# Top-16 attention scores as whole float32 products on half arrays, with the first values moved behind the first scores

## The chip, the cores and the metric

The kernel runs on one core of a Trainium2 chip. The metric is the device time of one execution in microseconds (us). PE is TensorE (PEld its weight loads), DVE is VectorE, ACT is ScalarE, POOL is GpSimd, SP is SyncE, which here only starts DMAs.

## The reference, cut to what matters

The whole computation is a small network on 1250 nodes and 512 features: a graph layer, a causal attention layer with experts, a second graph layer, and last a top-16 attention layer. Only the last one is touched:

```
x = x + (pos + pos_b)                      # depthwise taps along the rows
q, k, v = split(x @ qkv_w.T + qkv_b)       # 8 heads of 64
logits = einsum("bmd,bpd->bmp", q * scale, k)          # 1250 x 1250 for each head
_, idx = top_k(logits, 16)
attn = softmax(einsum("bmd,bmkd->bmk", q * scale, k[idx]))
out = einsum("bmk,bmkd->bmd", attn, v[idx]) @ wo_w.T + wo_b
```

Which 16 keys a row takes hangs on the exact order of its scores, so the scores need float32 precision.

## The kernel before

`top_layer` (from L1143) is the last of the kernel's stages and begins at about 1094 us of the profiled span. Its engines run programs of their own, which wait for each other on semaphores. After the taps, the q and k columns of the first pair of heads are projected (L1340), six chunks that ACT puts away in `QO` and `KT` (`keep_qk`, L1526). Then 80 tiles follow, n = 0 to 79: 8 heads of 10 tiles, and a tile is 128 queries against all 1250 keys. Two heads make a pair i; head `half` of the pair lies in rows 0 to 63 or 64 to 127 of `QO` and `KT`, since a head has 64 features. For each tile:

- PE `scores(n)` (L1373) makes 128 x 1250 scores in three PSUM banks; two sets of three banks alternate, so tile n needs ACT and DVE to be done with tile n-2.
- DVE `largest(n)` (L1678): the 8 largest, the scores without them, the next 8, the scores without those (four passes over 1250 columns, L1683 to L1691). After every second tile it takes a reciprocal of two sums (L1696), for which it waits on ACT's `total` (L1589).
- ACT: exp of the scores (L1581), exp of what is left (L1587), the sum (L1591); POOL subtracts the two (L1285), which leaves 16 weights a row. DVE may not overwrite its buffer of tile n before POOL has subtracted tile n-2.
- PE turns the weights by ten 128x128 transposes in three groups (L1406), each of which waits until ACT has put the group before it away (L1608), and for every second tile multiplies two tiles by the values (`weigh`, L1421, float32, output 64 wide, the two tiles on the two column halves of the array by turns).

PE, ACT and POOL walk the tiles in a written order. In PE's order round n is: first group of `turn(n-2)`, `scores(n+1)`, then a quarter of a job, second group, a quarter, third group, the rest. At every odd n there may be one job of the next pair (`work_at`, L1155): five q/k jobs of four 512-column products each, then three values jobs (four, four and two tiles of 128 rows; each is four products and one product with a single row for the bias, L1347 and L1349), 8 jobs in the 10 double rounds of a pair, three times. In the last 20 tiles only four light jobs are left. `weigh` comes in even rounds. I call two tiles (an odd round and the even one behind it) a round pair.

The scores need float32 precision, and the kernel gets it by splitting. k is staged twice over the 128 rows and split in a rounded part `kh` and a rest `kl`; q is stacked as rest and rounded part in `qs`. Then 128-row products of the type float32r over `kh` and over `kl` give the scores: 6 matmuls (512, 512, 226 columns, twice). The copies come by DMA (SP, L1231 to L1238, 4 of 320 KB for each head), and POOL splits them (`stage`, five operations for each head). For the first head that happens ahead of all scores: DVE splits k (L1673, L1675), POOL q. Meanwhile PE computes the first pair's values (L1368).

In the profile a float32 matmul leaves two MATMUL records, a transpose or a float32r matmul one.

Of the kernel before, what the change touches and what calls it, by code (L numbers as in the profile page):

```python
# [12 lines left out]
F32 = mybir.dt.float32  # L13
# [1129 lines left out]
def top_layer(nc, m, io, space, raw_qk, raw_v, taps, qb, s_ahead, ahead_done, out):  # L1143

    TN = H * NT
    LEFT, EXS, TOPS, PTS = 2, 3, 4, 4
    groups = pieces(NP)
# [7 lines left out]
    work_at, kept_after, jobs_before = {}, {}, {}  # L1155
    for i in range(1, HP):
        for v, job in enumerate(qk_jobs):
            work_at[2 * NT * (i - 1) + 1 + 2 * v] = ("qk", i, job)
        for v, ts in enumerate(v_groups):
            work_at[2 * NT * (i - 1) + 11 + 2 * v] = ("v", i, ts)  # L1160
# [8 lines left out]
    qk_kept = [None] + [kept_after[2 * NT * (i - 1) + 1 + 2 * (len(qk_jobs) - 1)] for i in range(1, HP)]  # L1169
    v_kept = [len(v_groups)] + [kept_after[2 * NT * (i - 1) + 11 + 2 * (len(v_groups) - 1)] for i in range(1, HP)]  # L1170
    qkv_jobs = jobs_before[61]

    with ExitStack() as ctx:
        s = Stage(nc, m, ctx, "tl")
        (s_zn, s_w_turned, s_w_kept, s_x_turned, s_x_kept, s_edge, s_tapped, s_mid, s_conv, s_first, s_first_kept,
         s_job, s_job_kept, s_wo_in, s_staged_k,
         s_fetched_0, s_fetched_1, s_staged, s_scored, s_max, s_negm, s_read, s_max2, s_topped, s_exp, s_rest,
         s_sum, s_inv, s_blank, s_probs, s_turned, s_kept, s_weighed, s_drained, s_normed, s_biased,
         s_projected, s_final, s_stored) = s.signals(
            "zn w_turned w_kept x_turned x_kept edge tapped mid conv first first_kept job job_kept wo_in staged_k "  # L1180
            "fetched_0 fetched_1 staged scored max negm read max2 topped exp rest sum inv blank probs turned kept "
# [11 lines left out]
        qs = space("tl_qs", 86016, [P, 2, NP], F32R)  # L1193
        kh = space("tl_kh", 96256, [P, 2, NP], F32R)
        kl = space("tl_kl", 106496, [P, 2, NP], F32R)
        qh = space("tl_qh", 116736, [P, NP], F32R)
# [18 lines left out]
        def logits(n):  # L1215
            return banks[:, 3 * (n % 2):3 * (n % 2) + 3, :].rearrange("p b c -> p (b c)")
# [10 lines left out]
        def _(sp):  # L1227
            sp.wait_ge(s_first_kept, 6)
            for i in range(HP):
                for half in range(2):  # L1230
                    r = slice(half * DH, (half + 1) * DH)  # L1231
                    if i:
                        sp.wait_ge(s_job_kept, qk_kept[i])
                        sp.wait_ge(s_scored, (2 * i + half - 1) * NT)
                    for arrived, rows in ((kl, KT[r, i % 2:i % 2 + 1, :]), (qs, QO[r, i:i + 1, :])):
                        for to in range(2):
                            sp.dma_start(arrived[to * DH:(to + 1) * DH, half:half + 1, :].bitcast(F32), rows
                                         ).then_inc(s_fetched[half], 16)  # L1238
                    if (i, half) == (3, 0):
                        sp.wait_ge(s_job, qkv_jobs)  # L1240
                        sp.dma_start(raw_wo[:, :, :], rows_of(io["L1_ffn_wo_w"])).then_inc(s_wo_in, 16)
            for half in range(2):
                sp.wait_ge(s_fetched[half], 64 * HP)
# [8 lines left out]
        def _(pool):  # L1252
            upper, lower = slice(0, DH), slice(DH, P)

            def stage(hi, step):

                half = hi % 2
                if step == (2 if hi == 0 else 0):
                    pool.wait_ge(s_fetched[half], 64 * (hi // 2) + 64)
                    if hi >= 2:  # L1260
                        pool.wait_ge(s_scored, (hi - 1) * NT)
                if step == 0:
                    op = pool.tensor_copy(kh[:, half, :], kl[:, half, :].bitcast(F32))
                elif step == 1:
                    op = pool.tensor_tensor(kl[:, half, :], kl[:, half, :].bitcast(F32),
                                            kh[:, half, :].bitcast(F32), ALU.subtract)
                elif step == 2:
                    op = pool.tensor_copy(qh[lower, :], qs[lower, half, :].bitcast(F32))
                elif step == 3:
                    op = pool.tensor_tensor(qs[lower, half, :], qs[lower, half, :].bitcast(F32),  # L1270
                                            qh[lower, :].bitcast(F32), ALU.subtract)
                else:
                    op = pool.tensor_copy(qs[upper, half, :], qs[upper, half, :].bitcast(F32))
                op.then_inc(s_staged, 1)
                pool.wait_ge(s_staged, 5 * hi + step - 1)

# [24 lines left out]
            for step in (2, 3, 4):  # L1301
                stage(0, step)
            for n in range(TN + 4):
# [6 lines left out]
                hi, step = (n + 8) // NT, (n + 8) % NT  # L1310
                if 0 < hi < 2 * HP and step < 5:
                    stage(hi, step)
# [5 lines left out]
        def _(pe):  # L1318
# [49 lines left out]
            for v, ts in enumerate(v_groups):  # L1368
                if v >= 2:
                    pe.wait_ge(s_job_kept, v - 1)  # L1370
                project_v(banks[:, 7 - v % 2, :], 0, ts).then_inc(s_job, 1)
# [25 lines left out]
            def turn(n, g):  # L1397
                if g == 0:
                    pe.wait_ge(s_probs, n + 1)
                    if n == 0:  # L1400
                        pe.wait_ge(s_job_kept, len(v_groups))
# [856 lines left out]
```

## Time and profile before

| | us |
|---|---|
| median of 3 runs | 1689.25 (1688.99 to 1690.77) |
| the profiled execution | 1686.05 |
| its span, first to last instruction | 1684.2 |
| first DVE pass over scores | 1146.81 |
| start of DVE's tile 79 | 1630.6 |
| mean granted TensorE clock | 0.966 |

The profiled execution is 1.85 us longer than its span and 3.2 us shorter than the median. The stretch that the change touches reaches from 1129 us to the end. A timeline row is a run of like instructions: start, time from the first start to the last end, engine, line, out<-in, rows*columns of the array, count, and in brackets the idle time before it with what ended it. The recorded end of a matmul lies behind the start of the next, since they are pipelined: for the pace, compare starts.

### The profile page before, as it was taken

How to read it: one execution, taken by the hardware profiler on the slowest of the kernel's cores; microseconds unless marked ns; L12 is line 12 of the kernel's file. 1: busy time of each engine (PE TensorE's matmuls, PEld its weight loads, DVE VectorE, ACT ScalarE, POOL GpSimd, SP SyncE). 2: the span in 40 equal slices, each digit the busy share in tenths (PEclk: the TensorE clock that was granted, in tenths of full speed). 3: DMA queues.
4: the chain of work that ended last, by engine and by line, in shares of the span. 5: the costliest groups of instructions: out<-in, count | busy, mean ns of one | idle time of the engine just before them, and what ended most of it. 6: DMA issues, size and time to landing. Idle time of an engine off the chain costs nothing. (4 is left out here: it accounts for less than half of the span.)

```text
span 1684.2 us, 22128 instructions
## 1 busy us (share of the span) xinstructions
PE 1486.9 (88%) x8227; PEld 928.2 (55%) x8227; DVE 1027.9 (61%) x2001; ACT 723.4 (43%) x1396; POOL 541.6 (32%) x399
## 2 busy tenths in 40 slices
PE   4888988997878789999999899777999999998778
PEld 2444534445666654454546545455776776776554
DVE  6999233327777721113223324748999999999981
ACT  4442013225565621111111220235778778778771
POOL 0113200015565410000000060007876667577550
PEclk9999989999999999999999999889999999999999
DMA  6001000025212050000000200011101100120001
GB/s 232 1 1 79 0 1 1 0 63 158 57 39 56 9 204 24 0 0 0 1 0 0 76 1 0 1 31 33 32 1 32 32 13 20 33 53 5 1 1 61
DMA packets 28570, 57.01 MB, mean 34 GB/s; under 512 B 7904, under 2 KB 12644, under 8 KB 28208
## 3 DMA queue, kind: packets, MB, share of 16 engines
q1 hardware_dynamic: 27152, 53.03, 11.5%
q10 hardware_dynamic: 1312, 2.56, 0.4%
q8 instruction: 68, 1.11, 0.3%
q14 instruction: 38, 0.31, 0.1%
HBM read 28.77 MB, written 5.84 MB: 21 GB/s over the span
## 5 line engine op out<-in xcount | busy, mean ns | idle before, releaser
L1285 POOL TENSOR_TENSOR tl_ex<-tl_ex,tl_left 128x1250 f32<-128x1250 f32 x80 | 209.8, 2622 | 37.0 <-ACT tl_left L1587 32.9
L1126 DVE SCALAR_TENSOR_TENSOR X<-ex_ps_x,g,X 128x512 f32<-128x512 f32 x80 | 59.9, 750 | 192.6 <-PE ex_ps_x L1019 192.6
L1406 PE MATMUL tl_banks<-identf,tl_ex 128*128 128x128 f32 x800 | 139.4, 290 | 42.1 <-ACT tl_pt L1608 25.6
L1608 ACT COPY tl_pt<-tl_banks 128x512 f32<-128x512 f32 (+1 forms) x200 | 108.1, 541 | 83.8 <-PE tl_banks L1406 80.8
L992 PE MATMUL ex_ps_h<-yt,w 128*128 128x512 f32 (+1 forms) x384 | 143.8, 529 | 0.0
L1406 PEld LDWEIGHTS tl_banks<-identf,tl_ex 128*128 128x128 f32 x800 | 90.0, 144 | 97.3 <-ACT tl_pt L1608 44.3
L1019 PE MATMUL ex_ps_x<-w,hid 128*128 128x512 f32 (+1 forms) x320 | 143.1, 599 | 0.0
L1072 ACT ACTIVATE hid<-ex_ps_h,b 128x512 f32<-128x512 f32 (+1 forms) x48 | 29.1, 608 | 242.2 <-PE ex_ps_h L992 242.2
L1899 POOL TENSOR_TENSOR lo<-xn,hi 128x512 f16<-128x512 f32 x5 | 5.9, 1186 | 379.5 <-ACT hi L1989 379.5
L1587 ACT ACTIVATE tl_left<-tl_left,tl_negm 128x1250 f32<-128x1250 f32 x80 | 107.5, 1343 | 29.2 <-DVE tl_left L1691 28.8
L1683 DVE MAX8 tl_m<-tl_banks 128x8 f32<-128x1250 f32 x80 | 116.3, 1454 | 5.7 <-PE tl_banks L1383 5.6
L1689 DVE MAX8 tl_m<-tl_left 128x8 f32<-128x1250 f32 x80 | 117.1, 1464 | 2.8
L1687 DVE MATCH_REPLACE8 tl_left<-tl_m,tl_banks 128x1250 f32<-128x1250 f32 x80 | 116.0, 1450 | 0.0
L1691 DVE MATCH_REPLACE8 tl_left<-tl_m,tl_left 128x1250 f32<-128x1250 f32 x80 | 115.6, 1445 | 0.0
L992 PEld LDWEIGHTS ex_ps_h<-yt,w 128*128 128x128 f32 x384 | 74.5, 195 | 65.8 <-issue 65.6
L1581 ACT ACTIVATE tl_ex<-tl_banks,tl_negm 128x1250 f32<-128x1250 f32 x80 | 104.7, 1309 | 2.4 <-DVE tl_left L1687 1.3
L1421 PE MATMUL tl_banks<-tl_pt,tl_V 128*64 128x128 f32 x1600 | 104.8, 278 | 0.0
L1019 PEld LDWEIGHTS ex_ps_x<-w,hid 128*128 128x128 f32 (+1 forms) x320 | 60.3, 189 | 74.0 <-issue 73.9
L1421 PEld LDWEIGHTS tl_banks<-tl_pt,tl_V 128*64 128x64 f32 x1600 | 85.7, 137 | 14.2 <-issue 14.2
L264 DVE TENSOR_SCALAR hot_m<-ruler,ends 128x240 f16<-128x240 f16 x323 | 92.6, 287 | 0.2 <-issue 0.2
L1340 PE MATMUL tl_banks<-tl_ct,tl_wt 128*128 128x512 f32 (+1 forms) x192 | 82.0, 554 | 9.3 <-DVE tl_ct L1658 6.2
L624 PE MATMUL ca_banks<-wqkv,ht 128*128 128x512 f32 x160 | 76.6, 625 | 12.7 <-DVE ht L804 12.7
(272 smaller groups left out, 2935.5 us busy)
## 6 DMA issues: line engine op xcount, KB each, us to landing
kl<-KT SPq DMA_DIRECT2D x16, 320.0 KB, 4.4
qs<-QO SPq DMA_DIRECT2D x16, 320.0 KB, 5.8
tl_kl<-tl_KT SPq DMA_DIRECT2D x16, 320.0 KB, 4.3
tl_qs<-tl_QO SPq DMA_DIRECT2D x16, 320.0 KB, 5.7
w<-in_L_ffn_W SPq DMA_DIRECT2D x8, 512.0 KB
w<-in_L_ffn_W SPq DMA_DIRECT2D x4, 1024.0 KB, 9.7
at_kept<-AT SPq DMA_DIRECT2D x1, 3200.0 KB, 10.9
AT<-at_kept SPq DMA_DIRECT2D x1, 3200.0 KB, 18.3
```

Of the source, the lines that this page charges most:

```text
L992: mm = pe.matmul(h_bank(u)[:, 0:w], w1[e][:, k, j * P:(j + 1) * P], yt[:, G % 2, k, 0:w], start=(k == 0), stop=(k == KD - 1))
L1019: mm = pe.matmul(x_bank(v)[0:rows(t), :], hid[:, (EX * G + e) % HIDS, j, r * P:r * P + rows(t)], w2[:, 2 * e + j, :], start=(j == 0), stop ...
L1285: pool.tensor_tensor(ex[:, n % EXS, 0:N], ex[:, n % EXS, 0:N], left[:, n % LEFT, :], ALU.subtract).then_inc(s_probs, 1)
L1406: mm = pe.transpose(ps_t[:, b * P:(b + 1) * P], ex[:, n % EXS, a + b * P:a + (b + 1) * P], m.identf[:, :])
L1421: mm = pe.matmul(ps_o[u * DH:(u + 1) * DH, 0:P], V[:, h // 2 % 2, k, h % 2 * DH:(h % 2 + 1) * DH], pt[:, (2 * j + u) % PTS, k * P:(k + 1) ...
L1581: act.activation(ex[:, n % EXS, 0:N], logits(n)[:, 0:N], ACT.Exp, bias=negm[:, n:n + 1]).then_inc(s_exp, 1)
L1587: act.activation(lf, lf, ACT.Exp, bias=negm[:, n:n + 1]).then_inc(s_rest, 1)
L1608: act.copy(pt[:, n % PTS, a:a + w], ps_t[:, 0:w]).then_inc(s_kept, 1)
L1683: dve.max(m8[:, n % TOPS, 0:8], logits(n)[:, 0:N]).then_inc(s_max, 1)
L1687: dve.match_replace(lf, m8[:, n % TOPS, 0:8], logits(n)[:, 0:N], TAKEN).then_inc(s_read, 1)
L1689: dve.max(m8[:, n % TOPS, 8:16], lf).then_inc(s_max2, 1)
L1691: dve.match_replace(lf, m8[:, n % TOPS, 8:16], lf, TAKEN).then_inc(s_topped, 1)
```

## The change

The scores are whole float32 matmuls with 64 rows, straight from `QO` and `KT`. Three matmuls a tile: keys 369 to 880 (512 columns) on the half of the array in which the head does not lie, from copies `qd` and `kd` that SP fetches crosswise for a pair at once (4 DMAs for a pair, two slots), and keys 0 to 368 and 881 to 1249 (369 columns each) on the head's own half. Each goes to a bank of its own. The first three tiles (`ALONE`) take all three matmuls on the own half and so need no copy. Splitting on POOL and DVE, and `kh`, `kl`, `qs`, `qh` are gone. The values of the first pair stand behind the scores in rounds 0 to 2, and the jobs of pair 1 begin at round 3 where they began at round 1; the later jobs keep their rounds.

```diff
+    ALONE = 3
+    SIDE = (N - BANK) // 2
...
+        at = 2 * NT * (i - 1) + (3 if i == 1 else 1)
+        for job in qk_jobs:
+            work_at[at] = ("qk", i, job)
+            at += 2
...
+            return banks[:, 3 * (n % 2):3 * (n % 2) + 3, :].rearrange("p b c -> p (b c)")[:, BANK - SIDE:BANK - SIDE + N]
...
+                if i:
+                    sp.wait_ge(s_job_kept, qk_kept[i])
+                if i >= 2:
+                    sp.wait_ge(s_scored, 4 * NT * (i - 1))
+                for copy, rows in ((kd, KT[:, i % 2:i % 2 + 1, :]), (qd, QO[:, i:i + 1, :])):
+                    for half in range(2):
+                        sp.dma_start(copy[(1 - half) * DH:(2 - half) * DH, i % 2:i % 2 + 1, :],
+                                     rows[half * DH:(half + 1) * DH, :, :]).then_inc(s_fetched[i % 2], 16)
...
-            for step in (2, 3, 4):
-                stage(0, step)
...
-                if 0 < hi < 2 * HP and step < 5:
-                    stage(hi, step)
...
                 if n == 0:
-                    pe.wait_ge(s_staged_k, 2)
-                pe.wait_ge(s_staged, 5 * (n // NT) + 3)
+                    pe.wait_ge(s_first_kept, 6)
+                if n >= ALONE:
+                    pe.wait_ge(s_fetched[i % 2], 64 * (i // 2) + 64)
...
-                for part in (kh, kl):
-                    for a, w in pieces(N):
-                        mm = pe.matmul(logits(n)[:, a:a + w], qs[:, half, t * P:(t + 1) * P],
-                                       part[:, half, a:a + w], start=(part is kh), stop=(part is kl))
-                mm.then_inc(s_scored, 1)
+                for other, a, b in ((1, SIDE, SIDE + BANK), (0, 0, SIDE), (0, SIDE + BANK, N)):
+                    if n < ALONE:
+                        other = 0
+                    at = (half + other) % 2
+                    r = slice(at * DH, (at + 1) * DH)
+                    q, k = (qd[r, i % 2, :], kd[r, i % 2, :]) if other else (QO[r, i, :], KT[r, i % 2, :])
+                    mm = pe.matmul(logits(n)[:, a:b], q[:, t * P:(t + 1) * P], k[:, a:b], start=True, stop=True)
+                    if a:
+                        mm.then_inc(s_scored, 1)
...
                 if n + 1 < TN:
                     scores(n + 1)
+                if n < len(v_groups):
+                    first_v(n)
                 if n in work_at:
...
                 if n < TN:
                     exponentials(n)
+                if n < len(v_groups):
+                    keep_first_v(n)
...
-            dve.wait_ge(s_fetched[0], 64)
-            dve.tensor_copy(kh[:, 0, :], kl[:, 0, :].bitcast(F32)).then_inc(s_staged_k, 1)
-            dve.wait_ge(s_staged_k, 1)
-            dve.tensor_tensor(kl[:, 0, :], kl[:, 0, :].bitcast(F32), kh[:, 0, :].bitcast(F32), ALU.subtract
-                              ).then_inc(s_staged_k, 1)
```

On PE at the first tiles, the program of before goes from the last projection of q and k through all of the values (L1347 with 128x128 outputs, L1349 the bias) to the scores of tiles 0, 1 and 2. Its last rows there:

```order
L1347 MATMUL tl_banks<-tl_wt,tl_ct 128x128 x4
L1349 MATMUL tl_banks<-v_b,ones 128x128
L1383 MATMUL tl_banks<-tl_kh,tl_qs 128x512 x2
L1383 MATMUL tl_banks<-tl_kh,tl_qs 128x226
L1383 MATMUL tl_banks<-tl_kl,tl_qs 128x512 x2
L1383 MATMUL tl_banks<-tl_kl,tl_qs 128x226
```

The changed program there, from the last projection of k to the first values (L1314 projects q and k, L1363 makes scores, L1321 and L1323 values):

```order
L1314 MATMUL tl_banks<-tl_ct,tl_wt 128x256 x8
L1363 MATMUL tl_banks<-tl_KT,tl_QO 128x512
L1363 MATMUL tl_banks<-tl_KT,tl_QO 128x369 x2
L1363 MATMUL tl_banks<-tl_KT,tl_QO 128x512
L1363 MATMUL tl_banks<-tl_KT,tl_QO 128x369 x2
L1321 MATMUL tl_banks<-tl_wt,tl_ct 128x128 x4
L1323 MATMUL tl_banks<-v_b,ones 128x128
```

The scores of tiles 0 and 1 moved ahead of the ten tiles of values; four of those stand between the scores of tiles 1 and 2, four behind tile 2's, two behind tile 3's.

In the middle, PE's order in an odd round with a q or k job, in the program of before:

```order
L1406 MATMUL tl_banks<-identf,tl_ex 128x128 x4
L1383 MATMUL tl_banks<-tl_kh,tl_qs 128x512 x2
L1383 MATMUL tl_banks<-tl_kh,tl_qs 128x226
L1383 MATMUL tl_banks<-tl_kl,tl_qs 128x512 x2
L1383 MATMUL tl_banks<-tl_kl,tl_qs 128x226
L1340 MATMUL tl_banks<-tl_ct,tl_wt 128x512
L1406 MATMUL tl_banks<-identf,tl_ex 128x128 x4
```

and in the changed one:

```order
L1386 MATMUL tl_banks<-identf,tl_ex 128x128 x4
L1363 MATMUL tl_banks<-tl_kd,tl_qd 128x512
L1363 MATMUL tl_banks<-tl_KT,tl_QO 128x369 x2
L1314 MATMUL tl_banks<-tl_ct,tl_wt 128x512
L1386 MATMUL tl_banks<-identf,tl_ex 128x128 x4
```

The place in the round is the same; only the matmuls that make the scores differ, and the rows of the array that they take.

## Rows read from the trace of the kernel before

**Rows 1.** Chain of waits, 1128 to 1150 us: start, us, what
```profile
1128.91 0.48 ACT tl_KT L1532
...
1129.41 0.47 SPq L1237
...
1131.63 6.25 DMA tl_qs<-tl_QO
...
1138.00 1.84 POOL tl_qh L1268
...
1139.91 4.03 POOL tl_qs L1270
...
1143.99 1.25 POOL tl_qs L1273
...
1145.38 1.40 PE tl_banks L1383 x6
...
1146.81 1.48 DVE tl_m L1683
```

**Rows 2.** Groups of DVE, 1146.8 to 1637 us: busy, mean ns, idle before
```profile
L1683 DVE MAX8 tl_m<-tl_banks 128x8 f32<-128x1250 f32 x80 | 116.3, 1454 | 5.7 <-PE tl_banks L1383 5.6
...
L1696 DVE RECIPROCAL tl_inv<-tl_rsum 128x2 f32<-128x2 f32 x39 | 6.1, 157 | 6.8 <-ACT tl_e L1591 6.8
```

**Rows 3.** Timeline of DVE: start, us, line, what, idle before it
```profile
1195.18 1.46 DVE L1683 MAX8 tl_m<-tl_banks 128x8 f32<-128x1250 f32 x1
...
1207.22 1.46 DVE L1683 MAX8 tl_m<-tl_banks 128x8 f32<-128x1250 f32 x1
...
1236.06 1.45 DVE L1691 MATCH_REPLACE8 tl_left<-tl_m,tl_left 128x1250 f32<-128x1250 f32 x1
1239.49 0.17 DVE L1696 RECIPROCAL tl_inv<-tl_rsum 128x2 f32<-128x2 f32 x1 [1.99 <-ACT tl_e L1591]
```

**Rows 4.** Timeline of PE, one round with a q or k job
```profile
1195.01 0.65 PE L1392 MATMUL tl_banks<-identf,tl_inv 128*64 128x128 f32 x4
1195.59 1.98 PE L1340 MATMUL tl_banks<-tl_ct,tl_wt 128*128 128x512 f32 x4
...
1197.77 0.81 PE L1383 MATMUL tl_banks<-tl_kh,tl_qs 128*128 128x512 f32 x3
1198.41 0.73 PE L1383 MATMUL tl_banks<-tl_kl,tl_qs 128*128 128x512 f32 x3
1198.99 0.60 PE L1406 MATMUL tl_banks<-identf,tl_ex 128*128 128x128 f32 x4
1199.51 1.31 PE L1421 MATMUL tl_banks<-tl_pt,tl_V 128*64 128x128 f32 x20
...
1209.52 0.81 PE L1383 MATMUL tl_banks<-tl_kh,tl_qs 128*128 128x512 f32 x3
```

**Rows 5.** Timeline of PEld: weight loads in that round
```profile
1204.14 0.73 PEld L1340 LDWEIGHTS tl_banks<-tl_ct,tl_wt 128*128 128x128 f32 x4 [0.27 <-ACT tl_ot L1617]
```

**Rows 6.** Timeline of PE, one round with a values job
```profile
1223.67 0.81 PE L1383 MATMUL tl_banks<-tl_kh,tl_qs 128*128 128x512 f32 x3
...
1230.05 1.16 PE L1347 MATMUL tl_banks<-tl_wt,tl_ct 128*128 128x128 f32 x8
1231.14 0.48 PE L1349 MATMUL tl_banks<-v_b,ones 1*128 1x128 f32 x2
1231.55 0.66 PE L1406 MATMUL tl_banks<-identf,tl_ex 128*128 128x128 f32 x4
...
1237.81 0.81 PE L1383 MATMUL tl_banks<-tl_kh,tl_qs 128*128 128x512 f32 x3
```

**Rows 7.** Timeline of PE while the staging runs
```profile
1130.11 1.16 PE L1347 MATMUL tl_banks<-tl_wt,tl_ct 128*128 128x128 f32 x8
...
1131.61 1.16 PE L1347 MATMUL tl_banks<-tl_wt,tl_ct 128*128 128x128 f32 x8
```

**Rows 8.** Busy time by stretch: PE, PEld, DVE, ACT, POOL, granted clock
```profile
1267.30:1387.80 120.50, 114.52 (x882) 85.92 (x880) 116.23 (x128) 94.62 (x177) 82.69 (x59) 0.99 0.09 19
```

More of the change, by code:

```diff
@@ L1155, in top_layer @@
     work_at, kept_after, jobs_before = {}, {}, {}
+    qk_done = [None]
     for i in range(1, HP):
[L1157 to L1160, printed above, removed]
+        at = 2 * NT * (i - 1) + (3 if i == 1 else 1)
+        for job in qk_jobs:
+            work_at[at] = ("qk", i, job)
+            at += 2
+        qk_done.append(at - 2)
+        for ts in v_groups:
+            work_at[at] = ("v", i, ts)
+            at += 2
     for b in range(KD):
@@ L1168, in top_layer @@
             evictions += len(work_at[n][2]) if work_at[n][0] == "qk" else 1
[L1169 to L1170 removed]
+    qk_kept = [None] + [kept_after[n] for n in qk_done[1:]]
     qkv_jobs = jobs_before[61]
@@ L1175, in top_layer @@
         (s_zn, s_w_turned, s_w_kept, s_x_turned, s_x_kept, s_edge, s_tapped, s_mid, s_conv, s_first, s_first_kept,
-         s_job, s_job_kept, s_wo_in, s_staged_k,
-         s_fetched_0, s_fetched_1, s_staged, s_scored, s_max, s_negm, s_read, s_max2, s_topped, s_exp, s_rest,
+         s_job, s_job_kept, s_wo_in,
+         s_fetched_0, s_fetched_1, s_scored, s_max, s_negm, s_read, s_max2, s_topped, s_exp, s_rest,
          s_sum, s_inv, s_blank, s_probs, s_turned, s_kept, s_weighed, s_drained, s_normed, s_biased,
          s_projected, s_final, s_stored) = s.signals(
-            "zn w_turned w_kept x_turned x_kept edge tapped mid conv first first_kept job job_kept wo_in staged_k "
-            "fetched_0 fetched_1 staged scored max negm read max2 topped exp rest sum inv blank probs turned kept "
+            "zn w_turned w_kept x_turned x_kept edge tapped mid conv first first_kept job job_kept wo_in "
+            "fetched_0 fetched_1 scored max negm read max2 topped exp rest sum inv blank probs turned kept "
             "weighed drained normed biased projected final stored")
@@ L1229, in _ @@
             for i in range(HP):
[L1230 to L1241, printed above, removed]
+                if i:
[6 more added lines that the diff above has]
+                                     rows[half * DH:(half + 1) * DH, :, :]).then_inc(s_fetched[i % 2], 16)
+                if i == 3:
+                    sp.wait_ge(s_job, qkv_jobs)
+                    sp.dma_start(raw_wo[:, :, :], rows_of(io["L1_ffn_wo_w"])).then_inc(s_wo_in, 16)
             for half in range(2):
-                sp.wait_ge(s_fetched[half], 64 * HP)
+                sp.wait_ge(s_fetched[half], 64 * HP // 2)
             sp.wait_ge(s_wo_in, 16)
@@ L1252, in _ @@
         def _(pool):
[L1253 to L1275, printed above, removed]
             def negate(n):
@@ L1543, in keep_job @@
                     if i >= 2:
-                        for half in range(2):
-                            act.wait_ge(s_fetched[half], 64 * (i - 1))
+                        act.wait_ge(s_scored, 4 * NT * (i - 1))
                     for name, c in what:
```

20 lines of the change are left out of this document (8 added, 12 removed).

## Prediction

> **What bounds the kernel now.** I read the chain of waits first, then DVE's groups, then the timelines. The chain [rows 1] shows what stands between the projections and the 80 tiles: ACT puts the last piece of k away until 1129.39, SP issues copies, they land at 1137.88, POOL splits q until 1145.24, PE makes the first scores (1.40), and DVE starts at 1146.81. From then on DVE is the pace: 80 tiles of four passes with 5.6 us of idle at the very start and only 6.8 us at the reciprocals [rows 2]. Undisturbed, two tiles take DVE 1207.22 - 1195.18 = 12.04 us [rows 3]. But PE is close behind: 114.5 of 120.5 us busy over the second pair of heads, at a granted clock of 0.99, the 2.4 GHz level [rows 8]. A round pair with a q or k job takes PE 1209.52 - 1197.77 = 11.75 us, 0.27 of it a wait for ACT [rows 4, 5], so 11.48 of work. One with a values job of four tiles takes 1237.81 - 1223.67 = 14.14, which is 2.1 more than DVE's 12.04 [rows 6]. There DVE does wait: 1.99 us ahead of the reciprocal at 1239.49, since ACT's sum stands behind copies that wait for PE [rows 3]. That is one of six such waits, two for each block of jobs, 2.3 a block.
>
> **The change part by part.**
>
> *The start.* SP's copies, POOL's 1.84 + 4.03 + 1.25 us and DVE's splitting leave the path. Scores of tile 0 can begin at 1129.4: 0.11 weights (half of the 0.20 switch below), then 1250 columns in two records each, all on one half. Price of a column: four records of 512 columns last 1.98, four of 128 last 0.65 [rows 4], so 1.33 us for 1536 columns more, 0.87 ns; at two cycles of the 2.4 GHz level it would be 0.83. I take 0.84: 2.10 us. With 0.19 from the last start to DVE's, DVE begins at about 1131.8 instead of 1146.81: **-15.0 us**. Bounds -14.8 (0.87 ns) and -15.1. The copies for tile 3 still land at about 1137.9 and are wanted 17 us after DVE's start, so they are hidden with 11 us to spare; SP has nothing else queued. Later pairs' copies are issued when k of the pair is put away, eight tiles (48 us) ahead. DVE and POOL drop work otherwise off the path: no gain.
>
> *The moved values.* One tile of values costs PE 1131.61 - 1130.11 = 1.50 us [rows 7]. Call DVE's start T. PE has scores 0 and 1 done at T+1.9, four tiles of values until T+8.0, scores 2 until T+10.3 (wanted at T+12, ready), four tiles until T+16.4. ACT is in order: its copy of those values waits for PE until T+16.5, and behind it are queued the exp of tile 1's rest (1.3), one copy of turned weights (the first transposes wait for the values too) and tile 1's sum, done at T+19.2. DVE wants that sum at T+18: **1.1 us** late. PE's tile 4 scores stand behind the transposes of tile 1, which wait for tile 0's third group, two tiles of values and ACT: I get T+27.1 against T+25.3, **2 us**; and tile 3's sum is late once more by **1.1**. Together +4.3; bounds +3 and +6, as every wait has a copy of 0.5 us as its grain.
>
> *The scores in the rounds.* Before: from kh's first start to the next transposes 1198.99 - 1197.77 = 1.22, of which 0.08 is the start of the first record (three of kh last 0.81, of kl 0.73): 1.14 [rows 4]. After, three terms. (a) The own half: 738 columns in two records, 1.24 us; the other half's 512 columns, 0.86, lie beside it if halves run at once. The trace has no two row halves at work, but two column halves: the 20 records of 128 columns of L1421 last 1.31, four records of L1392, all on one half, 0.65 [rows 4]. With 0.109 a record, L1392 is 4 x 0.109 + 0.21; L1421 less 0.21 is 1.10, ten slots for 20 records: pairs at once. Nearest row, so I take it for row halves. Bounds: 1.24 (at once) and 2.10 (one after the other, as in tile 0). (b) Changing the shape of the array. The one-row products of L1349 do it: L1347's eight records of 128 take 1231.14 - 1230.05 = 1.09 to the next start, 8 x 0.11 = 0.89 of it work: 0.20; L1349's two take 1231.55 - 1231.14 = 0.41 for 0.22 of work: 0.19 [rows 6]. (c) Back to transposes, whose weight loads are short: nearest is L1392, with short weights too, 1195.59 - 1195.01 = 0.58 for 0.44 of work: 0.15 [rows 4]. So 0.20 + 1.24 + 0.15 = 1.59 against 1.14: **+0.45 a tile, +0.9 a round pair**. Bounds +0.2 (switches hidden under weight loads) and +1.3 (halves in turn).
>
> *What the rounds do with it.* The wait of 0.27 goes under the longer scores. A q/k pair then takes 11.48 + 0.9 = 12.38, 0.34 over DVE; a values pair 14.14 - 0.2 + 0.9 = 14.8, +2.8; the short values pair (two tiles, 3 us of PE instead of four products of 0.86) 12.4, +0.4. Round pairs without a job have 2.5 us to spare. A block is 5 q/k, 2 values and 1 short pair: 1.7 + 5.6 + 0.4 = 7.7 us over. Block 1 starts with DVE already waiting for PE, so it pays all: 7.7. Only one free round pair lies ahead of block 2, two ahead of block 3; before, 4.2 us of excess cost 2.3 of waits, so the buffers absorb about 1.9, a bit more when refilled. I take 6.0 and 5.0. Sum 18.7, less 6.8 that is paid now: **+11.9**. Bounds +5 and +20. The last block and the tail behind tile 79 (1630.6 to 1684.2) have PE slack or are the same work; they move as a whole.
>
> **Sum**: -15.0 + 4.3 + 11.9 = +1.2 on the execution of 1686.05; on the median 1689.25 + 1.2 = **1690.5**. The change moves 15 us out of the start and PE gives them back in slices, by the values it now computes inside the rounds and by slower scores. 0.1 us on one tile's scores is worth 0.2 in each of 24 round pairs, 4.8 us: the sign hangs on that.
>
> **Rivals.**
>
> *Cheap switches (faster).* If a switch of shape costs half (0.10), scores are 1.41, +0.54 a round pair. q/k pairs are 12.02, just under DVE; values pairs 14.5, 2 x 2.5 less 1.9 absorbed is 3.1 a block: 9.3 - 6.8 = +2.5. The start gives -15.0 + 3.3. Sum -9, **1680**. For it: weight loads of a half might run under the transposes. Against: L1349's rows pay the full 0.2 each way.
>
> *Passes in program order (slower).* A float32 matmul has two records. If the own half's first record may not start before the other half's second one, it starts 0.43 late: 1.67 instead of 1.24. Round pairs grow by another 0.85: q/k +1.2, values +3.6, short +1.3, 14.5 a block; nothing is absorbed, since PE is late throughout: 43.5 - 6.8 = 36.7, plus 5 - 15.0: +27, **1716**. It decides from the point where a q/k pair passes 12.04. Against it stands L1421's count: in order it would need eleven slots, 1.42, and it has 1.31 [rows 4]. The Trainium skill, "TensorE: Matmul & The Clock Gate", section "The mechanism" of the part on packing, says that matmuls start and end strictly in program order; by that rule this rival would be the forecast. The trace has its doubt in one slot of 0.11 us, and on column halves only.
>
> *Halves in turn (the change doesn't do what it says).* 2.10 us a tile, +1.31: q/k pairs 14.1, values 16.5, short 14.1: 10.3 + 8.9 + 2.1 = 21.3 a block, 64 - 6.8 + 5 - 15 = +47, **1736**. Against it: L1421.
>
> *A dearer start or chain.* As forecast, but +0.2 us a tile from late second weight loads or ACT's copies: +5 to +14, **1698**. Nothing in the rows asks for it, but the forecast has no reserve for it.
>
> **How the numbers follow.** Forecast 0.53 (own range 1684 to 1697), cheap switches 0.20, dearer chain 0.15, program order 0.08, in turn 0.04. 0.2% is 3.4 us, about what a measurement of this kernel can tell from no change. Faster (below 1685.9): 0.19 of the cheap case and 0.09 of the forecast, 0.28. Within 0.2%: 0.33 of the forecast and 0.01 of the cheap case, 0.34. Slower: 0.11 of the forecast and the three dearer cases, 0.38. The range 1679 to 1712 leaves out the lower third of the cheap case, most of program order, and halves in turn: 0.07 + 0.07 + 0.04, about 0.2.
>
> **What would show it.** DVE's first pass at about 1131.8; two waits at the reciprocal and one for scores in the first five tiles, 4.3 in all; the three score matmuls with two records each, the own half's first starting within 0.01 us of the other's; 1.6 us from the first score start to the start behind; waits at reciprocals of 18 to 19 us over three blocks. Wrong: if q/k round pairs stay at 12.04 (switches cheap), or grow past 13 (order or turn). If PE's granted clock falls, all of PE's terms grow. If DVE's first pass isn't 15 us earlier, the first step fails.

## The result and the profile after

| | before | after |
|---|---|---|
| median, us | 1689.25 (1687.4 to 1690.8, 5 runs) | 1697.6 (1694.2 to 1701.6, 6 runs) |
| the profiled execution | 1686.05 | 1698.24 |
| its span | 1684.2 | 1696.1 |
| k of the first pair put away | 1129.39 | 1132.04 |
| first DVE pass over scores | 1146.81 | 1134.55 |
| start of DVE's tile 79 | 1630.6 | 1640.89 |
| from there to the end | 53.5 | 55.2 |
| mean granted TensorE clock | 0.966 | 0.966 |

A sixth run of the kernel before took 2983.76 us and is left out of its median. The changed kernel is slower by 0.5%: ratio 1.0049, 95% interval 1.0033 to 1.0065. The forecast was 1690.5 with a range of 1679 to 1712. The time lies inside, 7 us above the forecast, on the dearer side.

The start is as announced. The chain of waits of the changed kernel (start, us, what) goes from k straight to the scores; copies and POOL are off it, where [rows 1] had them for 16 us:

```profile
1127.64 3.90 PE tl_banks L1314 x17
...
1131.56 0.48 ACT tl_KT L1514
...
1132.18 4.43 PE tl_banks L1363 x12
```

The timeline of DVE has the first pass 2.51 us behind k:

```profile
1134.55 1.47 DVE L1661 MAX8 tl_m<-tl_banks 128x8 f32<-128x1250 f32 x1 [12.77 <-PE tl_banks L1363]
```

DVE's groups from 1134.5 us on show what it is paid with. They answer [rows 2]: the idle time at the reciprocals was 6.8 and is 24.6, and scores come late for 3.2 us more (16.0, of which 12.8 is the row above):

```profile
L1661 DVE MAX8 tl_m<-tl_banks 128x8 f32<-128x1250 f32 x80 | 116.6, 1457 | 16.1 <-PE tl_banks L1363 16.0
...
L1674 DVE RECIPROCAL tl_inv<-tl_rsum 128x2 f32<-128x2 f32 x39 | 6.3, 161 | 24.6 <-ACT tl_e L1573 24.6
```

One round pair with a q or k job in PE's timeline, for [rows 4]. The rows of the other half (64x512) and of the own half (64x369) start 0.01 us apart and lie over each other; the next kind of work starts 1.45 us behind them, and the round pair takes 1183.11 - 1170.66 = 12.45:

```profile
1170.66 0.69 PE L1363 MATMUL tl_banks<-tl_kd,tl_qd 64*128 64x512 f32 x1
1170.67 0.88 PE L1363 MATMUL tl_banks<-tl_KT,tl_QO 64*128 64x369 f32 x2
1171.20 0.59 PE L1363 MATMUL tl_banks<-tl_kd,tl_qd 64*128 64x512 f32 x1
1171.39 0.78 PE L1363 MATMUL tl_banks<-tl_KT,tl_QO 64*128 64x369 f32 x2
1172.11 0.66 PE L1386 MATMUL tl_banks<-identf,tl_ex 128*128 128x128 f32 x4
...
1183.11 0.69 PE L1363 MATMUL tl_banks<-tl_kd,tl_qd 64*128 64x512 f32 x1
```

Two records of the own half start before the second record of the other half's matmul, which stands ahead of them in the program. The Trainium skill, "TensorE: Matmul & The Clock Gate", section "The mechanism" of the part on packing, says matmuls start in strict program order. The first records do (1170.66, then 1170.67). The second record of the matmul in front, at 1171.20, does not come ahead of the own half's; for it, on two row halves, the trace does not agree.

The values pairs, one short pair and the free pair behind it, from the same view:

```profile
1220.46 0.69 PE L1363 MATMUL tl_banks<-tl_kd,tl_qd 64*128 64x512 f32 x1
...
1235.30 0.69 PE L1363 MATMUL tl_banks<-tl_kd,tl_qd 64*128 64x512 f32 x1
...
1250.14 0.69 PE L1363 MATMUL tl_banks<-tl_kd,tl_qd 64*128 64x512 f32 x1
...
1262.96 0.69 PE L1363 MATMUL tl_banks<-tl_kd,tl_qd 64*128 64x512 f32 x1
...
1271.19 0.44 PE L1386 MATMUL tl_banks<-identf,tl_ex 128*128 128x128 f32 x2 [0.68 <-ACT tl_pt L1590]
...
1273.14 1.09 PE L1386 MATMUL tl_banks<-identf,tl_ex 128*128 128x128 f32 x4 [0.93 <-ACT tl_spread L1588]
1274.16 1.22 PE L1363 MATMUL tl_banks<-tl_kd,tl_qd 64*128 64x512 f32 x1
...
1380.02 0.69 PE L1363 MATMUL tl_banks<-tl_kd,tl_qd 64*128 64x512 f32 x1
...
1390.76 0.69 PE L1363 MATMUL tl_banks<-tl_kd,tl_qd 64*128 64x512 f32 x1
```

A values pair takes 14.84, twice; the short one 12.82; and this free pair 11.20, of which PE waits 0.68 and 0.93 for ACT. Its end meets a fall of the granted clock: its last four transposes (1273.14) take 1.02 to the next start, where the same four take 0.56 elsewhere. At full clock a free pair takes 1390.76 - 1380.02 = 10.74, and so do the three others ahead of and behind block 3. Busy time by stretch around the fall:

```profile
1269.00:1273.00 4.00, 2.54 (x16) 1.24 (x12) 3.93 (x6) 3.46 (x9) 3.32 (x3) 1.00 0.00 0
1273.00:1277.00 4.00, 3.86 (x13) 2.17 (x13) 3.93 (x6) 2.22 (x4) 2.40 (x1) 0.57 0.00 0
```

The free pair of before, the same two waits in it, took 1260.36 - 1250.04 = 10.32:

```profile
1250.04 0.81 PE L1383 MATMUL tl_banks<-tl_kh,tl_qs 128*128 128x512 f32 x3
...
1257.92 0.44 PE L1406 MATMUL tl_banks<-identf,tl_ex 128*128 128x128 f32 x2 [0.70 <-ACT tl_pt L1608]
...
1259.87 0.84 PE L1406 MATMUL tl_banks<-identf,tl_ex 128*128 128x128 f32 x4 [0.93 <-ACT tl_spread L1606]
1260.36 1.39 PE L1383 MATMUL tl_banks<-tl_kh,tl_qs 128*128 128x512 f32 x3
```

One thing was not in the sum. In the start-up the granted clock falls (busy time by stretch of the changed kernel, columns as in [rows 8]), and tile 4's scores (second fence, PE's timeline) take 1163.17 - 1160.42 = 2.75 where tile 5's took 1.45:

```profile
1150.00:1157.00 7.00, 6.23 (x40) 4.54 (x39) 5.75 (x7) 2.59 (x5) 3.87 (x3) 1.00 0.00 0
1157.00:1164.00 7.00, 4.93 (x17) 2.39 (x15) 3.71 (x4) 4.33 (x8) 2.82 (x1) 0.74 0.00 0
1164.00:1172.00 8.00, 8.00 (x28) 4.03 (x26) 5.26 (x6) 4.90 (x8) 3.01 (x3) 0.80 0.00 0
```

```profile
1160.42 1.59 PE L1363 MATMUL tl_banks<-tl_KT,tl_QO 64*128 64x369 f32 x2
...
1163.17 2.07 PE L1314 MATMUL tl_banks<-tl_ct,tl_wt 128*128 128x512 f32 x2
```

**One table for all kernels.** "Late at n" is how far the start of DVE's first pass of tile n lies behind tile 0's start plus n times 6.025 us, DVE's pace in undisturbed stretches of both kernels. Tiles 5, 21, 41 and 61 end the start-up and the three blocks of jobs. One profiled execution each, from DVE's timeline (k from ACT's).

```
                          k put   first   late at tile                      79 to  
                          away    pass     5     21     41     61     79     end
before                   1129.39  17.42   0.0   3.0    5.4    7.9    7.9   53.5
after                    1132.04   2.51   7.7  15.9   24.5   30.4   30.4   55.2
x1 values ahead          1132.59  16.64   0.0   7.3   14.3   20.2   20.1   55.1
x2 move only             1131.66  18.40   4.0  10.4   13.3   15.7   15.7   54.2
x3 halves in turn        1135.07   2.51  11.5  34.4   63.1   91.6  112.0   60.0
x4 one more shape        1128.25   2.83   8.7  21.9   36.9   50.7   52.0   58.5
f1 first head only       1131.60   2.52   7.7  15.3   17.8   20.3   20.3   55.2
f2 f1, values spread     1131.30   2.52   7.7  14.8   16.1   18.0   18.0   54.2
b1 before, spread        1136.65  17.37   0.0   0.7    0.9    2.9    2.9   56.6
a1 after, spread         1130.37   2.52   7.6  16.2   23.5   30.5   30.5   55.2
g1 f2, staging later     1131.40   2.52   7.7  11.3   12.6   14.6   14.6   54.3
g2 g1, two tiles alone   1131.88   2.51   5.2   8.7    9.9   11.7   11.7   57.9
g3 after, jobs later     1134.24   2.52   5.4  14.5   22.8   30.2   30.2   55.2
a2 after, two alone      1136.19   2.51   3.5  11.8   20.4   26.3   26.3   53.5
("first pass": us from k put away to DVE's first pass)
```

For the two kernels of this case it adds up: +2.65 (k put away) - 14.9 (start) + 7.7 (start-up) + 22.7 (blocks) - 7.9 (what before paid) + 1.7 (behind tile 79) = +11.95, the difference of the spans. The first and the last of these are not the change's. The code up to k is the same in all fourteen kernels, and k is put away anywhere from 1128.25 to 1136.65; behind tile 79 it is 53.5 to 60.0. That is also why the medians differ by 8 and the two profiled executions by 12. Of the other kernels, too, read small differences with care: the kernel before, measured beside them, had medians of 1688.80, 1688.15, 1687.85 and 1687.89, so a ratio compares better than two medians.

### The profile page after: what moved, and what is told of

Read it like the earlier page. It is cut to its first block and busy times, and to the rows that moved or that the text cites. A ratio compares the mean times of both kernels' runs of the same rounds, so it can differ in the third digit from the quotient of the medians.

```text
span 1696.1 us, 22061 instructions
## 1 busy us (share of the span) xinstructions
PE 1516.9 (89%) x8227; PEld 904.0 (53%) x8227; DVE 1027.3 (61%) x1999; ACT 723.0 (43%) x1396; POOL 466.6 (28%) x361
## 5 line engine op out<-in xcount | busy, mean ns | idle before, releaser
L1363 PE MATMUL tl_banks<-tl_KT,tl_QO 64*128 64x369 f32 (+1 forms) x326 | 127.7, 514 | 0.7 <-ACT tl_KT L1514 0.7
L1363 PE MATMUL tl_banks<-tl_kd,tl_qd 64*128 64x512 f32 x154 | 90.2, 667 | 0.0
```

Of the source, the lines that this page charges most:

```text
L1363: mm = pe.matmul(logits(n)[:, a:b], q[:, t * P:(t + 1) * P], k[:, a:b], start=True, stop=True)
```

## The experiments

The theory: DVE gets an early start and PE takes it back, because values and dearer scores now lie inside rounds in which PE is the bound. Its rivals: the moved values alone do it; the granted clock does it; the two halves don't overlap to any use.

**x1: undo the move.**

```diff
-        at = 2 * NT * (i - 1) + (3 if i == 1 else 1)
+        at = 2 * NT * (i - 1) + 1
...
+            for v in range(len(v_groups)):
+                first_v(v)
...
-                if n < len(v_groups):
-                    first_v(n)
```

> The changed kernel with the move alone undone: the first pair's ten tiles of values stand ahead of the scores again and the jobs of pair 1 begin at round 1; the scores stay whole float32 products on half arrays. Theory (the rounds give the start back: slower scores cost about 0.45 us a tile in 24 round pairs, and the early start is worth having only with the move): PE has the values until 10 x 1.50 us after k is put away, so DVE starts about 12 us later than in the changed kernel, near 1147; the start-up delay of 7.7 us goes with it, the three blocks still cost about 8, 8 and 6 us: +4 to +8 against the changed kernel, about 1704, that is +12 to +16 against the kernel before. Rival (the moved values are what costs, the scores nothing): about the time of the kernel before plus 0 to 3, 1690 to 1693. Rival (the granted clock at the start is the cost): the three blocks would cost little more than 7.8 in sum here, since DVE starts late and PE is fed as before, about 1692.

Measured: 1700.95, ratio to before 1.0067 (1.0047 to 1.0088), 3.3 above the changed kernel, where I had expected 4 to 8, and 12.2 above the kernel before. Chain of waits:

```profile
1146.90 2.31 PE tl_banks L1366 x6
1149.23 1.48 DVE tl_m L1663
```

The first pass comes 16.64 behind k, so the start's gain is gone; and with DVE on time at tile 5, the blocks still cost 7.3, 7.0 and 5.9. So the slower scores cost some 12 us against the kernel before with no moved values at all, and both rivals that lay the cost on the start fall. The early start itself is worth only 3 us to the changed kernel: 14.1 us gained, 7.7 lost in the start-up and 2.5 more in blocks 1 and 2 (3.9 by the table, 3.3 by the medians).

**x2: the move alone, in the kernel before.**

```diff
+        at = 2 * NT * (i - 1) + (3 if i == 1 else 1)
...
                 if n + 1 < TN:
                     scores(n + 1)
+                if n < len(v_groups):
+                    first_v(n)
```

> The kernel before with the move alone: the first pair's values stand behind the first scores and the jobs of pair 1 begin at round 3; split products, copies and splitting stay. Theory: the start is still set by the copies and by POOL's splitting of q, so DVE begins at about 1147 as before and nothing is gained; the moved values delay the first tiles by 4 to 8 us, and block 1 has no spare round pair in front: +4 to +8 against the kernel before, 1694 to 1698. Rival (DVE has room for the values, the start-up delay of the changed kernel is all from its slower scores): +0 to +2, 1690 to 1692. Also to be read: whether the granted clock dips to below 0.8 in the first four tiles here too.

Measured: 1697.07, ratio 1.0046 (1.0031 to 1.0062). Values then no longer lie under the staging, PE has nothing to do from k on, and the granted clock is down when the scores come. Chain of waits and one stretch:

```profile
1146.18 1.25 POOL tl_qs L1277
...
1147.57 4.58 PE tl_banks L1388 x12
```

```profile
1140.00:1150.00 10.00, 2.43 (x7) 2.07 (x8) 3.25 (x2) 0.00 (x0) 7.07 (x3) 0.50 0.50 112
```

Two tiles take 4.58 where one took 1.40 in [rows 1]. Start-up 4.0, as expected; but block 1 costs 6.4 where it cost 3.0, which I had not foreseen. f1 shows why, below.

**x3: halves in turn.**

```diff
-                    if n < ALONE:
-                        other = 0
+                    other = 0
```

> The changed kernel with all three score matmuls of every tile on the head's own half of the array, one after the other; copies and waits stay. Theory (in the changed kernel two halves really work at once, and PE is what the 24 round pairs with jobs wait for): a tile's scores take 2.10 us in place of 1.24 and the two shape changes stay, +0.86 a tile, +1.7 a round pair, 24 of these make +41, and a few us for round pairs that had slack: +38 to +50 against the changed kernel, 1736 to 1748. Rival (the halves do not overlap to any use, and the three matmuls come one after the other anyway): within 5 us of the changed kernel.

Measured: 1787.25 (2 runs), 90 above the changed kernel. The halves do overlap in the changed kernel; the rival falls. The size is twice what I expected. Each q/k pair costs 1.7 more (late at 6, 8, 10: 11.8, 13.9, 16.0), 41 for 24 pairs, as worked out. On top, the free pairs now exceed DVE's pace too (12.45 from tile 37 to tile 39, where the changed kernel has 10.74), and the granted clock falls; what each of these adds was not separated. Two tiles' scores of the last rounds, and stretches of time in those rounds:

```profile
1697.21 2.36 PE L1362 MATMUL tl_banks<-tl_KT,tl_QO 64*128 64x512 f32 x6
...
1703.80 4.53 PE L1362 MATMUL tl_banks<-tl_KT,tl_QO 64*128 64x512 f32 x6
```

```profile
1664.00:1668.00 4.00, 2.81 (x14) 1.40 (x12) 3.77 (x4) 2.45 (x6) 2.75 (x3) 1.00 0.00 0
1668.00:1670.00 2.00, 1.69 (x5) 1.05 (x6) 1.93 (x4) 2.00 (x5) 0.42 (x1) 0.62 0.00 0
1670.00:1680.00 10.00, 10.00 (x57) 6.38 (x55) 7.39 (x8) 3.57 (x6) 2.68 (x3) 0.56 0.00 0
...
1720.00:1730.00 10.00, 10.00 (x42) 6.04 (x44) 7.29 (x8) 4.31 (x8) 2.61 (x2) 0.50 0.01 2
```

The same six records took 2.36 and 4.53, close to 1:2, the 2.4 and the 1.2 GHz level. The clock fell at 1668 to 1670, behind two waits of PE for ACT of 0.68 and 0.81 us, and stayed down for most of the next 10 us, in which PE was busy throughout. From tile 61 on, 20.4 us are lost in x3, and none in the changed kernel.

**x4: one more change of shape per tile.**

```diff
+                pe.matmul(banks[:, 3 * (n % 2), 0:8], m.ones[0:1, :], m.v_b[0:1, 0:8], start=True, stop=True)
                 for other, a, b in ((1, SIDE, SIDE + BANK), (0, 0, SIDE), (0, SIDE + BANK, N)):
```

> The changed kernel plus one matmul of one row and 8 columns ahead of the scores of every tile, into columns of PSUM that nobody reads: one more change of the array's shape for each tile, next to no work. Theory (a change of shape costs about 0.2 us, as the bias product's row shows, and each 0.1 us on a tile is worth 4.8 us of the whole): +0.2 to +0.25 a tile, +10 to +13 against the changed kernel, 1708 to 1711. Rival (the change of shape is free or hidden under weight loads, and the slower scores are due to their columns alone): +0 to +2, 1698 to 1700. Rival (PE is not what the rounds wait for): no difference.

Measured: 1721.49, ratio 1.0196 (1.0163 to 1.0228), 24 above the changed kernel: about twice what I had expected. PE's timeline:

```profile
1193.65 0.60 PE L1387 MATMUL tl_banks<-identf,tl_ex 128*128 128x128 f32 x4
1194.18 0.38 PE L1357 MATMUL tl_banks<-v_b,ones 1*128 1x8 f32 x2
1194.49 0.69 PE L1364 MATMUL tl_banks<-tl_kd,tl_qd 64*128 64x512 f32 x1
```

A product of one row and 8 columns takes 1194.49 - 1194.18 = 0.31 to the next start, with almost no work in it, and a q/k pair lasts 0.62 longer (late at 6, 8, 10: 8.7, 9.7, 10.7). That fits a dear change of shape, but which part of the 0.31 is the product's own was not separated. PE is what the rounds wait for; and 0.31 a tile is worth 21.6 us at tile 79, some 7 for each 0.1, not 4.8. Of the 21.6, 15 is 24 pairs, 1.0 the start-up, and 1.9 is that the three free pairs ahead of blocks 2 and 3, now 11.37, give back 0.6 less each. Behind the free pairs the granted clock falls again, for longer (0.50 to 0.52 from 1276 to 1282): the pair from tile 21 takes 15.99, the next 13.07. The rest of the 21.6, some 4, I put down to that. The Trainium skill, "TensorEngine Tiling (Array Packing)", section "Key Properties", says that changing the tiling mode drains TensorE; the row fits that and gives it a price of at most 0.31 us, though it does not show a drain as such.

**f1, f2: the slower scores for the first head alone.** The first head, which wants the early start, keeps the half-array products; the other seven take the split ones back. f2 also leaves a free round pair between the two full values jobs.

```diff
+                if n < NT:
+                    for other, a, b in ((1, SIDE, SIDE + BANK), (0, 0, SIDE), (0, SIDE + BANK, N)):
...
+                    return
                 for part in (kh, kl):
```

```diff
-        for ts in v_groups:
+        for at, ts in zip(((13, 17, 19), (31, 35, 39), (51, 55, 57))[i - 1], v_groups):
             work_at[at] = ("v", i, ts)
-            at += 2
```

> A mixture: the first head (tiles 0 to 9) is scored by whole float32 products on half arrays as in the changed kernel, the other seven heads by the split products of the kernel before with their copies and POOL's splitting; the move of the first values stays. Theory (the early start is worth 15 us less the start-up delay of about 8, and what gives it back is the slower scores in 24 round pairs): DVE starts at about 1132 to 1135, start-up 8, block 1 about 5 to 6 (the first two or three round pairs with slow scores, no spare pair in front), blocks 2 and 3 as before at 2.8 and 2.5: 2 to 6 us under the kernel before, 1683 to 1687, and 10 to 14 under the changed kernel. Rival (the move and the granted clock at the start are the cost, and they stay here): at or above the kernel before, 1689 to 1697.

> The mixture plus a spare round pair between the two full values jobs of each block (values jobs at rounds 13, 17, 19; 31, 35, 39; 51, 55, 57). Theory (a values pair of 14.1 us on PE is 2.1 over DVE, a buffer of about 1.9 us takes it, and a spare pair fills it again): blocks 2 and 3 cost 0 to 0.6 in place of 2.8 and 2.5, block 1 gains 1 to 2: 4 to 7 under the mixture without it, 1678 to 1682. Rival (the buffer is not what takes it, the delay comes from ACT's order in that round and comes back each time): within 1 us of the mixture without it.

Measured: f1 1691.1, ratio 1.0020 (1.0010 to 1.0029): 6.5 under the changed kernel, but above the one before, a miss. f2 1685.0, ratio 0.9977 (0.9963 to 0.9992), 6 under f1, as expected, but not the 1678 to 1682 that built on f1's forecast. In f1 blocks 2 and 3 cost 2.5 each as before; the 7.7 of block 1 is what was missed. DVE's and POOL's timelines:

```profile
1233.37 0.09 DVE L1706 MATCH_VALUE_LOAD tl_left<-tl_m,tl_banks 128x8 f32 x1 [4.60 <-POOL tl_ex L1292]
```

```profile
1228.79 1.25 POOL L1270 CAST tl_kh<-tl_kl 128x1280 fp32r<-128x1280 f32 x1 [7.55 <-DVE tl_m L1702]
1230.13 0.22 POOL L1286 TENSOR_SCALAR tl_negm<-tl_m 128x1 f32<-128x1 f32 x1
```

The move puts k of pair 1 away one round pair later. POOL is in order and stands 7.55 us in front of the splitting that needs the copies of that k, with the negated maximum and the subtraction of the next tile behind it. (The profile names DVE as releaser, which had long been done; the copies were last.) This is x2's dear block 1 as well: there POOL stands 7.56 us in front of the same splitting, and DVE waits 3.00 and 0.57 behind it. The changed kernel has no splitting and is spared.

**b1, a1: spread the values jobs alone,** in the kernel before (11, 15, 19; then as in f2) and in the changed one.

> The kernel before with the values jobs spread alone (rounds 11, 15, 19; 31, 35, 39; 51, 55, 57). Its three blocks cost 2.3 to 2.9 us of DVE's time each, at the second full values job. Theory of the buffer of 1.9 us that a spare round pair fills: nearly all of 7.85 goes, -5 to -7: 1682 to 1684. Rival (a values job costs its wait whatever stands in front): 0 to -1, 1688 to 1689.

> The changed kernel with the values jobs spread in the same way (13, 17, 19; 31, 35, 39; 51, 55, 57). Here a round pair with a q or k job is itself 0.4 us over DVE and a values pair 2.8. Theory: block 1 has no spare pair before round 13, so it gains at most 1; in blocks 2 and 3 the spare pair between the values jobs fills the buffer and takes some 2 us each, but block 2 begins with the buffer spent: -2 to -5 against the changed kernel, 1693 to 1696. Rival (the granted clock decides, not the order): no difference from 1697.6 beyond 1 us.

Measured: b1 1687.59, ratio 1.0000 (0.9988 to 1.0011); a1 1696.41, ratio 1.0060 (1.0041 to 1.0078). In a1 the lateness at tile 79 is 30.5 against 30.4: nothing gained, the expectation fell, and so did b1's of 1682 to 1684. What a free pair saves at the values jobs, the q/k pairs behind it pay. b1 is odd: at tile 79 it is 4.95 us less late than before, as the buffer theory has it, and the median of 12 runs is the same as before within 0.1%. Its profiled execution is 5.3 longer in its span than that of before: k is put away 7.3 later and the part behind tile 79 takes 3.0 more, and neither is in the code that was changed. f1 is odd too: by its row (2.5 + 20.3 against 17.4 + 7.9) it is 2.5 better than before, by its median 3 worse, and the execution profiled was the fastest of its ten. So a gain of less than some 5 us in one row of the table need not show in the median. b1's runs have a lower mean granted clock (median 0.9625; 0.965 for the kernel before on the same chip), and among them time and clock go together, 1684.8 at 0.966 and 1694.2 at 0.958. Whether the order of jobs lowers the clock, and by what, was not tested; it stays open.

**g1, g2: the mixture mended.** g1 is f2 with POOL's splitting for the first head of pair 1 two tiles later; g2 is g1 with two tiles alone.

```diff
                 hi, step = (n + 8) // NT, (n + 8) % NT
+                if hi == 2:
+                    hi, step = (2, n - 14) if n >= 14 else (0, 0)
```

```diff
-    ALONE = 3
+    ALONE = 2
```

> The mixture with spread values jobs, and POOL's splitting of the third head (the first of pair 1) two tiles later. In the mixture DVE waited 4.60 us at 1228.8 to 1233.4: k of pair 1 is put away two rounds later than before, its copies landed about 8 us behind that, and POOL, which is in order, stood at the splitting with the negated maximum and the subtraction of the next tiles queued behind it. Theory: that wait goes, what is left there is the 0 to 1 of a values pair: 3 to 4.6 us less, 1680.5 to 1682. Rival (the wait only moves: PE is late by as much, as the values job stands there): 0 to -1, 1684 to 1685.

> The same with tile 2 scored on both halves (two tiles alone on the own half in place of three). Its scores come some 8 us behind the copies' landing by the trace, so the copies are there. It takes 0.86 us off PE in the start-up, in which PE is never idle for long. Theory (the start-up delay of 7.7 us is PE's work, by way of the buffers): -0.9 to -1.5 in the DVE starts of tiles 3 to 5, at the end of it 0 to -1.5 in the time. Rival (the start-up delay is set by ACT's order and by the granted clock, not by PE's work): no shift of tile 5's start beyond 0.3.

Measured: g1 1682.69, ratio 0.9976 (0.9963 to 0.9989), 2.3 under f2 where 3 to 4.6 was expected; lateness at tile 21 falls from 14.8 to 11.3, so the wait at POOL's splitting was real and, by this row, did not move elsewhere. g2 1679.09, ratio 0.9935 (0.9914 to 0.9956), the fastest of all and faster than both kernels of the case. Tile 5 starts 2.5 earlier for 0.86 us of PE's work, more than the 0.9 to 1.5 expected; the time, 3.6 under g1 where at most 1.5 was expected, falls by more than the table's 2.9.

**g3: the jobs of pair 1 two rounds later, in the changed kernel.**

```diff
-        at = 2 * NT * (i - 1) + (3 if i == 1 else 1)
+        at = 2 * NT * (i - 1) + (5 if i == 1 else 1)
```

> The changed kernel with the jobs of pair 1 at rounds 5 to 19 in place of 3 to 17: a free round pair behind the start, none between blocks 1 and 2. Theory (in the changed kernel PE's work is what the first 40 tiles wait for; PE's excess is kept whatever the order, only free pairs in which PE would stand idle give anything back): tile 5 starts about 2 to 3 us earlier against DVE's pace, tile 21 at the same place as before within 1, and the whole within 1.5 us of 1697.6. Rival (each part is a delay of its own: start-up, block, block): the start-up shrinks by 2 to 3 and that stays, 1694 to 1696. Also to be read: how long tile 4's scores last if no job stands behind them, and at which granted clock.

Measured: 1697.35, ratio 1.0050 (1.0033 to 1.0066), the changed kernel's time. Tile 5 is 2.3 us less late, tile 21 1.4, tile 61 0.2. Moved work is paid later, in full.

**a2: two tiles alone, in the changed kernel** (the line of g2).

> The changed kernel with two tiles alone on the own half in place of three, so tile 2 is scored on both halves: one line. In the mixture the same line took 2.5 us off the start of tile 5 (0.86 of PE's work, and a dip of the granted clock that met less of tile 4's scores), and that stayed to the end. Theory (PE's work is what the first 20 tiles wait for, and PE's work that is gone, unlike work that is moved, is not paid later): tile 5 starts 2.0 to 2.6 us earlier against DVE's pace, tile 20 too, the drift at the last tile is 28 in place of 30.4, and the time 1695 to 1696. Rival (block 1 takes up whatever the start-up gives back, as it did when the jobs were moved): tile 5 earlier, tile 21 not, 1697 to 1698.

Measured: 1692.77, ratio 1.0026 (1.0013 to 1.0040), 4.8 under the changed kernel. Work that is gone stays gone: 4.1 less late at tiles 5, 21, 41 and 79. That is more than the 2 to 2.6 I gave, and the profile says why. In this execution the granted clock did not fall in the start-up:

```profile
1157.00:1164.00 7.00, 4.93 (x33) 3.83 (x34) 6.03 (x7) 3.32 (x5) 3.13 (x3) 1.00 0.00 0
1164.00:1172.00 8.00, 8.00 (x34) 3.91 (x31) 5.99 (x6) 5.79 (x12) 5.82 (x4) 1.00 0.00 0
```

```profile
1163.71 0.69 PE L1363 MATMUL tl_banks<-tl_kd,tl_qd 64*128 64x512 f32 x1
...
1165.15 1.13 PE L1314 MATMUL tl_banks<-tl_ct,tl_wt 128*128 128x512 f32 x2
```

Tile 4's scores take 1.44 here. g2, with the same start and a clock of 0.76 from 1157 to 1164, is 5.2 late at tile 5, this one 3.5. The same work, from tile 4's first score to tile 5's, takes 6.97 in a2 (1163.71 to 1170.68), 8.63 in g2 and 10.24 in the changed kernel (1160.42 to 1170.66). So the clock is worth 1.7 in g2 and 3.3 in the changed kernel, where it fell for all of tile 4. In each of the five profiled executions with three tiles alone and a job in round 3 (after, f1, f2, a1, g1) this stretch takes 10.2, so the fall is not one execution's bad luck; with two tiles alone it came in g2 and not in a2, one execution each.

## Why the prediction came out as it did

- **The start, -15.0: right.** 17.42 became 2.51, -14.9. The copies landed under the first tiles' work.
- **The scores, +0.45 a tile: right.** q/k pair 12.45 (12.38 forecast), values pair 14.84 (14.8). Halves at once, with two changes of shape at full price. From the first score to the start behind, it is 1.45 and not the 1.6 announced, since the way in is paid ahead of it: the four transposes in front take 0.59 to the first score, where before they took 0.41. Cheap switches, program order and halves in turn are refuted by these rows; x3 and x4 measured what turns and one more switch would have cost.
- **The moved values, +4.3: the order was right, the size wrong, 7.7.** a2 at full clock is 3.5 late with 0.86 less of PE's work; 3.5 + 0.86 is 4.4. The remaining 3.3 is the granted clock, 0.74 and 0.80, as the stretch from tile 4's scores to tile 5's shows. The three waits came where they were announced, as 0.96, 3.25 and 2.90 for 1.1, 2 and 1.1. I had named a falling clock as what would upset the terms and given it no price. The dips of the kernel before stood in the same stretch of its trace (0.61 from 1150 to 1154, 0.57 from 1164 to 1168), where they cost nothing: DVE was not late up to tile 5.
- **The blocks, 7.7 + 6.0 + 5.0 = 18.7: too small, 8.2 + 8.6 + 5.9 = 22.7.** The step that failed is "Round pairs without a job have 2.5 us to spare". I took PE's work and left out what PE waits for ACT in such a pair, 0.68 and 0.93, which no slack removes. A free pair of the changed kernel takes 10.74 at full clock, so 1.3 is to be had. The pairs of a block as measured are 5 x 0.40 + 2 x 2.8 + 0.8 = 8.4 over DVE's 12.05. Block 3 has two free pairs ahead: 8.4 - 2.6 = 5.8, measured 5.9. Block 2 has one, which leaves 7.1. The other 1.5 is the granted clock, 0.57 from 1273 to 1277, right behind that free pair: the two pairs from tile 19 on take 11.20 and 13.57, 1.6 more than such pairs at full clock (10.74, and 12.44 as in x1 from tile 21). g3 has no free pair there and pays 8.3 in block 2. The short values pair was mis-summed besides: 12.38 less 3.44 for the four products plus 3.0 for two tiles is 11.9, not the 12.4 I wrote, and with ACT's 0.93 it is the 12.82 measured.
- **What before paid, 6.8: too small, 7.9.** I took the waits at the reciprocals alone; by DVE's starts the kernel before lost 7.9, so 1.1 more was to be set against the blocks.
- **The sensitivity, 4.8 us for 0.1 us a tile: too small.** x4 measured 7, of which some 1.2 I put down to the granted clock.
- **The tail, unchanged: right for the change.** 55.2 against 53.5 is the clock of that execution (0.97 behind tile 79, against 0.99); a2 has 53.5 with the same code.
- **The base.** I added +1.2 to an execution whose k was put away early, 1129.39 in a spread of 1128.25 to 1136.65. The difference was carried to the median, so this did no harm.

Together: the start missed by 0.1, the start-up by 3.4 and the blocks by 4.0, less 1.1 for what before paid: 6.4 in the 80 tiles, +7.6 where +1.2 was forecast. The median came out 7.1 above the forecast. That is the 1698 of the rival "a dearer start or chain", but by luck: it asked for 0.2 us more on each tile, and a tile's scores cost what was forecast. What was missed is the granted clock, some 4.9 us in start-up and block 2, and the two waits in the free pairs. The rows of the kernel before had both: dips in the start-up and waits of 0.70 and 0.93.

## What to carry to other kernels

When the bound moves from one engine to another, price the new bound by whole rounds, start to start with its waits, and not by its work; slack that consists of hand-offs can't be spent. Give a fall of the granted clock a price wherever PE will be the bound: here it was some 4.9 us, most of the miss. Move work off a start only into rounds that have room, and make the dear form of a product for the tiles alone that need it: here the first ten of eighty bring the early start, and the other seventy only paid. Work taken away is kept, work moved behind the bound is paid in full.

## What the runs showed of the hardware

- Two float32 matmuls of 64 rows on different halves of the array start 0.01 us apart, and records of the second start ahead of the first one's second record. All on one half, a tile's scores took 2.29 start to start (tile 2 of the changed kernel, 1142.55 to 1144.84); on two halves 1.45.
- A one-row, 8-column float32 product between products of other shapes costs 0.31 us.
- The granted clock differs where the work does not: g2 and a2 have the same order and the same waits of PE up to tile 4's scores, with a2 4.3 us later, and g2 had 0.76 from 1157 to 1164 us, a2 1.00 from 1161 to 1168. Where it fell in the changed kernel and in x3, PE had waited for ACT just before (0.68 and 1.39 us ahead of 1160; 0.68 and 0.93 ahead of 1273; 0.68 and 0.81 ahead of 1668). The same waits of 0.68 and 0.93 stand ahead of 1391 with no fall, and once down it stayed at 0.50 to 0.56 over 10 us in which PE was busy throughout (x3). What sets it was not found; fillers in PE's gaps were not tried, since no PSUM bank is free there.
